# A two-layer state-space and attention network on one core: the transposition of the maxima moves from the second to the third step of a half unit, the split of the maxima from the seventh to the eighth

## The reference, cut to what matters

```python
# attention layer, per batch
scores = jnp.einsum('bhtd,bhsd->bhts', q, k) / sqrt(HD)      # 512 x 512 per head
attn   = jnp.einsum('bhts,bhsd->bhtd', softmax(scores), v)
# node c, c = 0..5
q = ew[c,0] * (nodes[in_q] @ We[eq] + be[eq]);  k, v the same way
nodes[c] = act_w[c] * mha(q, k, v, Wq[c], Wk[c], Wv[c], Wo[c]) + q
```

## Time and profile before

| | |
|---|---|
| time, median of 3 runs | 2220.38 us (2218.78 to 2220.67) |
| the profiled execution's own time | 2223.95 us |
| its span | 2221.9 us |
| TensorE busy | 2039.9 us, 92% |
| VectorE busy | 1737.5 us, 78% |
| ScalarE busy | 1486.8 us, 67% |
| GpSimd busy | 341.7 us, 15% |

### The profile page before, as it was taken

One profiled execution on the slowest core, in us unless ns is written; L12 is line 12 of the kernel. 1 busy time (PEld: TensorE's weight loads), 2 busy tenths in 40 slices (PEclk: granted clock), 3 DMA queues, 4 the chain that ended last, 5 costly groups with the idle time before them and its releaser, 6 DMA issues.

```text
span 2221.9 us, 32029 instructions
## 1 busy us (share of the span) xinstructions
PE 2039.9 (92%) x10812; PEld 846.9 (38%) x10812; DVE 1737.5 (78%) x3501; ACT 1486.8 (67%) x2004; POOL 341.7 (15%) x385
## 2 busy tenths in 40 slices
PE   5748886999999999999999999999999999999995
PEld 2224443333333333444444444444444444443332
DVE  5856887788787877888888888888878888888884
ACT  4743453566666677777777777777777777776664
POOL 1101332000000011111111111111111111113223
PEclk9977786799999999999999999999999999999998
DMA  3001104233333355566566656556666566665630
GB/s 103 19 24 54 56 33 86 43 66 75 63 75 67 82 104 107 117 109 109 109 109 109 108 109 109 108 110 109 109 110 108 108 109 109 109 108 101 98 58 25
DMA packets 137197, 195.63 MB, mean 88 GB/s; under 512 B 20152, under 2 KB 55632, under 8 KB 137040
## 3 DMA queue, kind: packets, MB, share of 16 engines
q1 hardware_dynamic: 137040, 193.63, 45.5%
HBM read 75.45 MB, written 23.73 MB: 45 GB/s over the span
## 4 chain that ended last, share of the span: by engine, by line
PE 81%; DVE 13%; issue 4%; ACT 1%; POOL 1%; DMA 1%; DVEq 0%; POOLq 0%; SPq 0%; ACTq 0%
PE bank_s L1031 27%; PE bank_o L1069 22%; PE bank_x L1054 6%; DVE nm L1386 5%; PE bank_m L1082 3%; PE bank_x L1017 3%; PE bank_x L996 3%; PE bank_x L1004 2%; PE bank_m L1102 2%; PE bank_x L983 2%; PE bank_x L1128 2%; PE bank_s L934 1%; DVE big L1275 1%; PE bank_m L1092 1%; PE bank_m L1041 1%
## 5 line engine op out<-in xcount | busy, mean ns | idle before, releaser
L1386 DVE TENSOR_REDUCE nm<-bank_s 128x1 f32<-128x512 f32 x2048 | 1336.2, 685 | 342.3 <-PE bank_s L1031 341.4
L821 ACT ACTIVATE big<-bank_x 128x1024 f32<-128x1024 f32 x1024 | 1048.0, 1024 | 486.5 <-PE bank_x L1054 458.9
L1031 PE MATMUL bank_s<-kst,qst 62*128 62x512 f32 x2048 | 837.5, 469 | 53.1 <-DVE nm L1386 52.5
L1054 PE MATMUL bank_x<-qst,kst 64*128 64x512 f32 x2048 | 750.0, 447 | 1.6 <-ACT big L821 1.6
L1031 PEld LDWEIGHTS bank_s<-kst,qst 62*128 62x128 f32 x2048 | 358.9, 187 | 693.3 <-DVE nm L1386 609.4
L1069 PE MATMUL bank_o<-big,at 128*32 128x512 f32 x4096 | 556.4, 616 | 2.2 <-ACT big L821 2.0
L1054 PEld LDWEIGHTS bank_x<-qst,kst 64*128 64x128 f32 x2048 | 304.3, 187 | 10.2 <-issue 6.0
L605 POOL CAST at<-at 128x512 fp32r<-128x512 f32 x112 | 68.2, 609 | 1273.3 <-ACT at L752 1035.8
L607 POOL TENSOR_TENSOR at<-at 128x512 fp32r<-128x512 f32 x112 | 143.3, 1280 | 10.0
L1069 PEld LDWEIGHTS bank_o<-big,at 128*32 128x32 f32 x4096 | 81.2, 108 | 153.1 <-issue 149.2
L829 ACT ACTIVATE big<-bank_x,big 128x128 f32<-128x128 f32 x256 | 68.7, 376 | 27.3 <-issue 11.6
(11 more groups left out here) (154 smaller groups left out, 1511.4 us busy)
## 6 DMA issues: line engine op xcount, KB each, us to landing
at<-nodes_d SPq DMA_DIRECT2D x144, 256.0 KB, 5.9
kst<-at SPq DMA_DIRECT2D x288, 128.0 KB
qst<-at SPq DMA_DIRECT2D x288, 128.0 KB
nodes_d<-big SPq DMA_DIRECT2D x48, 256.0 KB, 3.1
at<-w_d SPq DMA_DIRECT2D x48, 193.0 KB, 5.8
at<-x2T_d SPq DMA_DIRECT2D x32, 256.0 KB, 4.4
kst<-at SPq DMA_DIRECT2D x128, 64.0 KB
qst<-at SPq DMA_DIRECT2D x128, 64.0 KB
```

The costliest lines, as they stand in the source:

```text
L821: act.activation(PT[:, kp, h, :, :], ring.take()[0].rearrange("p (c n) -> p c n", c=2), ACT.Exp, scale=x.c.scale).then_inc(S["c_ex"], 1)
L1031: pe.matmul(bank_s[:, n % 2, :], qst[rows, x.r, h, t * P:(t + 1) * P], kst[rows, x.r, h, :], start=True, stop=True).then_inc(S["c_s_ps"], 1)
L1054: mm = pe.matmul(sec(to, j), kst[rows, x.r, h, kc_ * P:(kc_ + 1) * P], qst[rows, x.r, h, :], start=True, stop=True)
L1386: dve.tensor_reduce(nm[:, k, at_n:at_n + 1], bank_s[:, n % 2, :], AX.X, ALU.max, negate=True).then_inc(S["c_red"], 1)
```

## The change

Three placements move, and no operation is added or removed. `maxima` on TensorE and `ev_m` on ScalarE go from step 1 of each half to step 2, behind that step's value or query projection and behind its copy. `parts` on VectorE goes from step 6 to step 7.

```diff
@@ ScalarE
                         if i == 1:
                             ev_pv(*((last, 1) if k == 0 else (x, 0)))
-                        if i == 1:
-                            ev_m(*led_group(c, q, r, k))
                         if k == 0:
                             if i == 2:
                                 ev_v(at_(c, q, r + 1))
+                                ev_m(*led_group(c, q, r, k))
...
                             if i == 2:
                                 ev_qT(ahead)
                                 ev_kh(only(ahead, False))
+                                ev_m(*led_group(c, q, r, k))
@@ TensorE
                         output(x, k, 0, i - 4)
-                        if i == 1:
-                            maxima(*led_group(c, q, r, k))
                         if i == 3:
                             turn(*((last, 1) if k == 0 else (x, 0)))
                         if k == 0:
                             if i == 2:
                                 value(at_(c, q, r + 1))
+                                maxima(*led_group(c, q, r, k))
...
                             if i == 2:
                                 proj_q(ahead)
                                 proj_kh(only(ahead, False))
+                                maxima(*led_group(c, q, r, k))
@@ VectorE
                             reduce(*group)
 
-                            if i == 6:
+                            if i == 7:
                                 parts(*read_group(c, q, r, k), j)
```

## The result

The change made the kernel slower: 2233.46 us (median of 4 runs, 2230.85 to 2236.7) against 2220.16 (4 runs), a ratio of 1.0064 with an interval of [1.0049, 1.0078] as recorded (the two medians by themselves divide to 1.0060). The forecast was 2224.9 with a range up to 2229. The profiled execution took 2236.7 us, of which 2234.7 are its span, so 12.8 us more than the span before.

What follows compares the result with a forecast made beforehand. The prediction took TensorE, busy 92% of the span, as the bound, with VectorE releasing some second tiles. Terms 0.17 + 0.015 - 0.075 = +0.11 us a node unit, times 40 = +4.4, gave 2224.9 us; range 2217.5 to 2229.

Steps and rivals of the forecast that it cites:

- Transposition, half 1: Node units, half 1, steps 1 and 2: moving the transposition opens a wait; 3.76 us against 3.59, +0.17 us a unit.
- The opened wait: Step 2 of half 1: second score tile, held by VectorE's chain through node_out, 0.41 us behind its pair; 0.17 us stall.
- The copy on ScalarE: Steps 2 and 3: the maxima's copy queues behind another copy and releases turn later; +0.015 us in half 1, 0 in half 0.
- a visible wait of turn for the copy: Step 3: turn visibly waiting for the maxima's copy would show the prediction wrong.
- The rival of the late copy: Without overlap of ScalarE copies, turn comes 0.05 and 0.11 us later; unit +0.26, total 2231 us; chance 0.12.
- Transposition, half 0: Node units, half 0, step 2: no node_out, second tile 0.21 us behind its pair, just free; 0, with 0.03 to spare.
- Split, half 1: VectorE's split of the maxima, step 6 to 7 of half 1: hidden beside TensorE's work in either step; 0.
- Split, half 0: Without the split's cast in step 6 of half 0, step 7's second tile loads earlier; -0.075 us a node unit.
- The law of the late tile: A second score tile up to about 0.24 us behind its pair is free; beyond, each 0.01 us costs 0.01.
- DMAs: A group's two DMAs leave SP up to 2 us later, with about 5 us to spare in half 0; 0.
- Elsewhere I take 0: Attention-layer units and the last seven units: the moved placements cost and gain nothing; 0.
- The sum: Node unit: 0.17 + 0.015 - 0.075 = +0.11 us; times 40 = +4.4; median 2224.9 us.

## Why the prediction was wrong

**Transposition, half 1: right.** The opened wait was forecast at 0.17 and measured 0.17 to 0.18, in the kernel after and by node_out in halves. Steps 1 and 2 took 3.66 us, not 3.76, for one reason: behind a projection the transposition costs 0.11, where the forecast carried over the 0.21 of step 1.

**The copy on ScalarE: the step that was mis-sized, +0.015 for +0.16.** Its place was right, its size not. Turn was put 0.80 us behind the start of step 3 and came at 0.97. Some 0.10 of this is the transposition's lower price: step 3 starts that much earlier than forecast, and ScalarE's row of copies does not. The rest is the release: from the end of a ScalarE copy to TensorE 0.11 to 0.14 us pass here (1200.09 to 1200.20 for turn's weight load; 1220.99 to 1221.13), and the forecast used the 0.05 it had read behind VectorE. With the 0.10 won in step 2 the two errors nearly cancel: +0.23 for half 1 instead of +0.185. The forecast had named a visible wait of turn for the copy as a sign that it is wrong, and so it came. The rival of the late copy had the wait, but not its cause: it took the copies not to overlap on ScalarE, and they still did, by 0.11 us (L742 ends at 1199.95, the maxima's copy starts at 1199.84).

**Transposition, half 0: 0, and 0 was measured**, though not as reasoned: step 2 gets 0.10 cheaper and turn's hold in step 3 takes 0.10.

**Split, half 1: the step that failed.** "Step 6 has a projection, so its cast lies beside TensorE's work; step 7, too, is long enough: **0**." It measured +0.28 a unit, 11.2 us in all. The step was checked against VectorE's own work and TensorE's, and not against GpSimd, which works on SBUF in that step and the two behind it. GpSimd held the cast and the subtraction there: in the run in which it waits for them the 0.28 is gone (step 1 of half 0 back at 1.66), with the split still in step 7.

**Split, half 0: -0.075 for 0, the second step that failed.** The law of the late tile was drawn through two points, and the second one, step 7, was held by ScalarE's copy (L797) as well, which released it within 0.03 us of the tile. The law itself held elsewhere (0.45 behind the pair: step 5 of half 1 0.17 longer; 0.52 behind: step 1 of half 0 0.28 longer; 0.60 behind with turn_ctx moved: step 7 at 2.08), so that its second point was right by luck; but at the step to which it was applied the tile was not alone.

**DMAs: 0**, as forecast: SP's queue and the DMAs hold 0% of the chain that ended last.

**"Elsewhere I take 0": wrong in both directions.** Attention-layer units of the two kinds took 28.50 and 26.05 us instead of 28.81 and 26.27, some 4.5 us over 17 units. With the transposition in step 2 of these units the layer took 470.4 to 475.5 us in ten profiles, and 484.2 to 488.3 in the three with it in step 1. What the units do not account for, 5 us or more, goes with less time at the lower clock in some (mean granted clock 0.98 in the kernel after against 0.96 before). Cut into 17 stretches of a unit's length from 419 us on (416 after), seven have a mean granted clock of 0.94 before and three after, and a stretch with such a clock takes 0.7 to 1.6 us more than its like. Why the shifted layer is granted more is not shown. The third stretch gained 3.25 through the split, as the run with the split alone shows. The last stretch cost 7.6 us in this one execution, at a lower clock; before and in ten of the eleven experiments' profiles it took 79.0 to 83.1 us, in one (transposition ahead, split in step 6) 86.65, so it goes with the single execution more than with the change.

**The sum.** Forecast 0.11 a node unit; measured 0.52. Of the 0.41 between them 0.05 is the copy and the transposition's price, 0.28 the split in half 1, 0.075 the gain that did not come. Over 40 units that is 16 us too little; the attention layer and the third stretch give 15 back, and the last stretch takes 7.6. The forecast of the median missed by 8.6 us through errors twice that size with opposite signs.

## What to carry to other kernels

Before an instruction of VectorE moves, look at what GpSimd does at its new place, and read the longest durations of that instruction in the trace before, not only its mean: here the wait for the other engine showed there and nowhere else. A late tile, or any wait, sets a step only if nothing else ends at the same time; a law from two points needs each point's own releaser. And when a small matmul is placed, read its price beside the neighbour that it will have: here the same 32-column transposition cost 0.21, 0.11 or 0.02 us, and the place at 0.02, with the split kept away from GpSimd and node_out in halves, made the kernel 1.1% faster than before (2195.72 us).

## What was not expected of the hardware

- VectorE's operations on 16 columns, 0.17 us alone, took 0.45 and 0.85 beside GpSimd's on 512, and ended within 0.03 us of them.
- A transposition with 32 columns of weights ahead of a matmul with 128: that matmul started 0.12 us behind it and the step grew by 0.02; ahead of matmuls with 32 columns it grew by 0.21.
- From the end of ScalarE's copy to the matmul that waits for it 0.14 us, from VectorE's reduction to a weight load 0.05.
